# Image 0 loaded as two half transfers on two queues, and seven more idle matmuls, in a one-core attention kernel

## The reference

```
# layer 0
xn  = group_norm(x, eps=1e-5) * gn_scale + gn_bias
q, k, v = split(xn @ w_qkv per head)            # 4 heads of 16 channels
att = softmax(q k^T * 64**-0.5)                 # 256 x 256 per image and head
x   = (att v) @ w_out + b_out + xn
# layer 1
xn  = group_norm(x, eps=1e-3) * gamma + beta
q, k, v = xn @ Wq + bq, xn @ Wk + bk, xn @ Wv + bv
att = softmax(q k^T * 64**-0.5)                 # one head
out = xn + (att v) @ Wp + bp
```

## Time and profile before

| | |
|---|---|
| Three runs | 52.26, 52.64 and 55.1 us, median 52.64 |
| The profiled execution's own time | 52.91 us |
| Its span, first to last instruction | 51.1 us |
| Mean granted TensorE clock | 0.993 of full speed |
| Busy: PE, DVE, ACT, POOL | 89%, 72%, 53%, 35% of the span |
| Input and output | 1.07 MB in all DMAs, 0.72 MB of them read from HBM |

### The profile page before, as it was taken

The page is one execution under the profiler, slowest core; times in us unless marked ns, Lnnn a source line. Parts: engine busy times, 40 slices in busy tenths (PEclk is TensorE's granted clock), DMA queues, the critical chain, the costliest instruction groups (busy, mean ns, idle before and its releaser), DMA issues.

```text
span 51.1 us, 1307 instructions
## 1 busy us (share of the span) xinstructions
PE 45.4 (89%) x459; PEld 38.5 (75%) x459; DVE 36.9 (72%) x102; ACT 27.1 (53%) x63; POOL 18.1 (35%) x44
## 2 busy tenths in 40 slices
PE   2999999789999999599999999995999999999900
PEld 2979979679778497457686687593989999999700
DVE  0047799939926999979999974899489969955330
ACT  0494094506897705910663499672795966343300
POOL 5797637988784000000004450627727000000000
PEclk9999999999999999999999999999999999999997
DMA  0387000000000000000000000000000001010101
GB/s 0 103 228 220 14 0 0 0 0 0 0 13 0 0 0 0 0 6 13 0 0 0 0 0 0 13 0 0 0 0 6 6 0 30 22 51 0 51 13 51
DMA packets 1255, 1.07 MB, mean 21 GB/s; under 512 B 160, under 2 KB 1056, under 8 KB 1248
## 3 DMA queue, kind: packets, MB, share of 16 engines
q1 hardware_dynamic: 1024, 0.82, 5.9%
q10 hardware_dynamic: 224, 0.16, 1.1%
HBM read 0.72 MB, written 0.26 MB: 19 GB/s over the span
## 4 chain that ended last, share of the span: by engine, by line
PE 78%; DVE 7%; ACT 4%; issue 3%; POOL 2%; POOLq 0%; DVEq 0%
PE bank L729 12%; PE bank L761 8%; PE bank L846 7%; PE bank L740 6%; PE bank L720 6%; PE bank L854 6%; PE bank L696 5%; PE bank L835 4%; PE bank L665 4%; PE bank L784 3%; ACT pt L437 3%; PE bank L776 3%; PE bank L816 2%; DVE mv L523 2%; PE bank L817 2%
## 5 line engine op out<-in xcount | busy, mean ns | idle before, releaser
L583 DVE TENSOR_REDUCE nmax<-bank 128x2 fp32r<-128x512 f32 x16 | 10.0, 678 | 2.7 <-PE bank L720 2.7
L437 ACT ACTIVATE pt<-bank 128x512 f32<-128x512 f32 x16 | 8.5, 594 | 5.4 <-PE bank L740 5.4
L333 POOL TENSOR_TENSOR rstd<-mv,half 64x1 f32<-64x1 f32 (+1 forms) x7 | 4.4, 633 | 15.2 <-DVE mv L523 14.8
L729 PE MATMUL bank<-ident,nmax 128*128 128x256 f32 x38 | 7.3, 308 | 0.0
L854 PE MATMUL bank<-idle 128*128 128x128 bf16 x59 | 6.4, 283 | 1.0 <-POOL idle L303 1.0
L729 PEld LDWEIGHTS bank<-ident,nmax 128*128 128x128 f32 x38 | 5.3, 188 | 1.7 <-issue 1.2
L854 PEld LDWEIGHTS bank<-idle 128*128 128x128 bf16 x59 | 5.5, 135 | 1.1 <-POOL idle L303 1.0
L720 PE MATMUL bank<-qk 32*128 32x256 f32 x32 | 3.3, 324 | 1.2 <-ACT pt L437 0.6
L761 PE MATMUL bank<-pt,v 128*32 128x256 f32 x64 | 4.3, 385 | 0.0
L846 PE MATMUL bank<-vn,pt 128*128 128x65 f32 x32 | 4.2, 273 | 0.0
L500 DVE BATCH_NORM_STATS2 bn<-xin 64x6 f32<-64x256 f32 x4 | 1.7, 418 | 3.3 <-DMA xin<-x_dram 3.3
(11 more groups left out here) (104 smaller groups left out, 119.2 us busy)
## 6 DMA issues: line engine op xcount, KB each, us to landing
par<-params_dram SPq DMA_DIRECT2D x1, 288.0 KB, 3.0
out_dram<-res SPq DMA_DIRECT2D x4, 64.0 KB, 1.5
xin<-x_dram SPq DMA_DIRECT2D x1, 128.0 KB, 2.9
par<-params_dram ACTq DMA_DIRECT2D x1, 96.0 KB, 2.9
par<-params_dram SPq DMA_DIRECT2D x1, 64.0 KB, 1.8
xin<-x_dram ACTq DMA_DIRECT2D x1, 64.0 KB, 2.3
xin<-x_dram SPq DMA_DIRECT2D x1, 64.0 KB, 2.7
```

What stands on the lines that cost most here:

```text
L333: nc.gpsimd.tensor_tensor(rstd[:, layer, a:z], mv[:, layer, a:z, 1], half[:, a:z], ALU.pow).then_inc(rstd_ready, 1)
L437: nc.scalar.activation(pt[:, b, h, :, :], bank("T", b, h)[:, :, :], ACT.Exp, scale=SCALE).then_inc(exp_done, 1)
L583: nc.vector.tensor_reduce(nmax[:, b, h, :], bank("S", b, h)[:, :, :], AX_X, ALU.max, negate=True).then_inc(s_max, 1)
L729: pe.matmul(o[:, :, t * HALF:(t + 1) * HALF], nm[:, t:t + 1].broadcast_to([128, 128]), ident[:, :].unsqueeze(1).broadcast_to([128, 2, 128] ...
```

## The change

Image 0 is no longer one transfer of 64 rows on ACT. Its channels 0 to 31 are the first transfer on SP and its channels 32 to 63 are the first on ACT; both add 16 to the same semaphore, so that everyone who waits for image 0 now waits for 32. Block A becomes the second transfer on SP, and images 1, 2 and 3 move back one place each; block B stays second on ACT behind a smaller one; block C still waits for image 0. The slices of image 1 and of images 2 and 3 are written with fewer dimensions. PE's stream gets 2 more idle matmuls between `hop(0)` and `hop(1)` (18 for 16), 1 more ahead of `qk_(0)` (5 for 4) and 4 more ahead of `hop(2)` (10 for 6). Two slices (`qk[:, b, 0:2, :]`, `kl[rows(h), b]`) name the same elements as before.

```diff
+X0_DONE = 32
...
         @block.sync
         def _(sp):
+            sp.dma_start(xin[0:C // 2, 0, :], x[0:C // 2, 0, :]).then_inc(x_in[0], 16)
             sp.dma_start(par[:, 0:END_A], params[:, 0:END_A]).then_inc(a_in, 16)
-            sp.dma_start(xin[:, 1:2, :], x[:, 1:2, :]).then_inc(x_in[1], 16)
-            sp.dma_start(xin[:, 2:B, :], x[:, 2:B, :]).then_inc(x_in[2], 16)
-            sp.wait_ge(x_in[0], 16)
+            sp.dma_start(xin[:, 1, :], x[:, 1, :]).then_inc(x_in[1], 16)
+            sp.dma_start(xin[:, 2:B, :].rearrange("c b n -> c (b n)"), x[:, 2:B, :].rearrange("c b n -> c (b n)")).then_inc(x_in[2], 16)
+            sp.wait_ge(x_in[0], X0_DONE)
             sp.dma_start(par[:, END_B:WIDTH], params[:, END_B:WIDTH]).then_inc(c_in, 16)
...
-                pool.wait_ge(x_in[chain_of(0, b)], 16)
+                pool.wait_ge(x_in[chain_of(0, b)], X0_DONE if b == 0 else 16)
...
-            act.dma_start(xin[:, 0:1, :], x[:, 0:1, :]).then_inc(x_in[0], 16)
+            act.dma_start(xin[C // 2:C, 0, :], x[C // 2:C, 0, :]).then_inc(x_in[0], 16)
...
-                act.wait_ge(x_in[chain_of(0, b)], 16)
+                act.wait_ge(x_in[chain_of(0, b)], X0_DONE if b == 0 else 16)
...
-                nc.scalar.copy(qk[:, b, :, :], bank("QK", b)[:, :, :]).then_inc(qk_hi, 1)
+                nc.scalar.copy(qk[:, b, 0:2, :], bank("QK", b)[:, :, :]).then_inc(qk_hi, 1)
...
-                dve.wait_ge(x_in[chain_of(0, b)], 16)
+                dve.wait_ge(x_in[chain_of(0, b)], X0_DONE if b == 0 else 16)
...
-                               kl[rows(h), b, :] if low else qk[rows(h), b, 1, :], start=(t == 0 and not low),
+                               kl[rows(h), b] if low else qk[rows(h), b, 1, :], start=(t == 0 and not low),
...
-            keep_warm(24); hop(0); keep_warm(16); hop(1); weights_vp(); keep_warm(4); qk_(0); v(0); y_input(0)
-            keep_warm(6); hop(2); keep_warm(7); attend(("S", 0, 0), ("S", 0, 1), ("S", 0, 2), ("S", 0, 3))
+            keep_warm(24); hop(0); keep_warm(18); hop(1); weights_vp(); keep_warm(5); qk_(0); v(0); y_input(0)
+            keep_warm(10); hop(2); keep_warm(7); attend(("S", 0, 0), ("S", 0, 1), ("S", 0, 2), ("S", 0, 3))
```

More of the change, by code:

```diff
@@ L225, in build @@
         dve_step = sem("dve_step")
-        read_by = {"S": s_max, "T": exp_done, "S1": s1_max, "T1": exp1_done, "WV": wvp_ready, "QK": k_ready,
+        read_by = {"S": s_max, "T": exp_done, "S1": s1_max, "T1": exp1_done,
+                   "WV": wvp_ready, "QK": k_ready,
                    "V": v_ready, "HOP": var_ready, "Y": xn1_ready,
```

## The result

The changed kernel takes 55.64 us (median of four executions: 55.43, 55.53, 55.76, 56.18) against 52.67 us before. The ratio is 1.061, with a 95% interval of 1.049 to 1.072. It is slower by 3 us where 0.1 us was forecast; the range ended at 53.5.

The account below looks back on a forecast made before the run. PE, busy 89% of the span, was taken to bound the kernel, with only the start movable. Start +0.12 us, the rest 0: 52.91 to 53.03 us profiled, median 52.76, stated as 52.7; range 52.1 to 53.5 us.

Parts of the forecast that it names:

- which wait takes over: Head of DVE's stream: the wait for block A ends last, swallowing image 0's gain; statistics start 0.12 us later.
- signs of being wrong: Profile signs: DVE idle over 0.3 us before image 1's statistics; idle matmuls' loads still 107 ns after 7.5 us; others.
- Block A was put at 1.17 plus 2.0: Block A second on SP: issued at 1.17, landing at 3.17 us, bounds 2.97 to 4.0.
- Image 1 was put at 4.15: Image 1 third on SP: lands at 4.15 us, half the extra issue's delay; variance of image 0 0.09 us later.
- image 1's slack: DVE ahead of image 0's variance: 0.16 plus 0.19 us of waiting, minus a few hundredths, taken to absorb a later image 1.
- rival D: Start of kernel: both halves and block A land together at about 3.05, image 1 uses its slack; 52.6 us, chance 0.15.
- The rule on partition halves: Splitting image 0: the skill's rule says no gain, later half at 3.05; the rows suggest up to half a microsecond.
- the cover of the idle matmuls at full clock: Seven added idle matmuls on PE: hidden behind other waits, cost 0, bounds 0 and 0.50 us.
- the later first hop: PE's hop of image 0: follows the spread statistics to 4.00 from 3.88, counted as 0.12 us of start delay.
- rival C: PE idles longer before image 0's hop, so its clock rises later: costs 1.46 us, time 54.1 us, chance 0.06.

Follow-up runs that it names:

- r8: Changed kernel with block A first on SP again and half of image 0 second: six executions at 52.68 to 52.95 us, two at 55.73 and 59.85; ratio 1.0038.
- r2: Kernel before with only the change's idle matmuls (18, 5, 10 for 16, 4, 6): 52.70 us, ratio 1.0006.
- r3: Changed kernel with 30 idle matmuls for 24 ahead of the first hop: 52.93, 53.18, 53.20 and 53.30 us, ratio 1.009.
- r12: Kernel before with 22 idle matmuls for 24 ahead of the first hop: two executions at 52.56 and 52.62 us, eight from 55.02 to 59.15 us.
- r1: Changed kernel's transfers with the idle matmuls of before (16, 4, 6): 55.15, 55.16, 58.57 and 59.28 us.
- r9: Changed kernel without DVE's head wait for block A, 26 idle matmuls for 24 before the first hop: seven executions at 52.71 to 53.25 us, three at 54.46 to 55.49.
- r6: Kernel before with 26 idle matmuls for 24 ahead of the first hop: eight executions at 52.43 to 52.74 us, two at 55.19 and 55.29.
- r4: Changed kernel without the wait for block A at the head of DVE's stream: 52.62, 54.33, 55.56 and 59.73 us.
- r5: Kernel before with 20 idle matmuls for 24 ahead of the first hop, no transfer moved: 54.60, 55.49, 58.97 and 59.03 us.

## Why the prediction was wrong

**Right: which wait takes over.** The prediction said that block A would end last at the head of DVE's stream and swallow the gain of image 0. It did; the bracket names `par`. Two of its signs of being wrong came as well: DVE idle for 0.37 us ahead of the statistics of image 1, and weight loads of idle matmuls above 100 ns after 7.5 us.

**Its size was too small.** Block A was put at 1.17 plus 2.0; it took 1.19 plus 2.3 in this execution and 2.0 to 2.3 in the seven traces with these transfers, so the 2.0 was their lower end. Image 1 was put at 4.15, with half of the extra issue counted; it came at 4.55, the full delay and a bit more. So the start cost 0.40 us at the variance for the predicted 0.12, and 0.51 us at the first scores with the gap filled. The halving of the delay because "the bytes ahead of it are the same ones as before" did not hold. Block B is issued sooner now (1.18 for 1.33) and may compete with image 1, but no run separates this. The prediction also took image 1's slack as 0.16 plus 0.19 us: the 0.16 is DVE already waiting for image 1, so only the 0.19 was slack, as its own 0.35 us for a landing at 4.4 has it, and rival D had less room than the 0.35 it counts on.

**The rule on partition halves.** By the Trainium skill, "DMA: Bandwidth & Descriptors", section "Rules for kernel authors", splitting by partition halves brings nothing. In the changed kernel the later half landed at 2.74 for 3.05, and in all seven traces with this order the halves took 1.7 to 2.1 us against 2.2 to 2.4 us for the 64 KB. But this order also moves block A, which was issued beside image 0 before, out of the first place; with A back in it (r8) the later half landed at 3.06, and nothing was left of the gain. So in these runs the 0.3 us came only together with the loss of block A's place. Whether two halves are faster by themselves no run separates. The two inputs that DVE needs together were complete at 3.49 instead of 3.05.

**Right: the cover of the idle matmuls at full clock.** Their cost was taken as 0 with a bound of 0.50; r2 measured 52.70 against 52.67.

**The step that failed: the later first hop was costed as a delay only.** The prediction put the hop 0.12 us later, carried that as 0.12 us of chain, and put its effect on the clock at nothing. Measured, the hop came 0.40 us later, and the clock, which had risen near 6 us, rose near 13 us, which made 2.45 of the 2.97 us (r3). The prediction did have the mechanism as rival C, a longer idle time of PE ahead of the first hop and a later rise, and gave it 0.06. It held against it that "the change adds idle matmuls in just this stretch". They are not in that stretch: all seven stand behind the first hop, while the gap is ahead of it. The three executions of before already held a 55.1, and I named it under rival C without reading it as a sign that the kernel stands at an edge; eight of its 65 executions are beyond it, and eight of ten with 0.2 us more of gap. The two errors belong together: had the hop come only 0.12 us later, the idle time would have been some 0.50 us (an estimate from 0.38), between r8 (0.46, 2 of 8 late) and r12 (0.57, 8 of 10 late), and the median could have fallen on either side.

**Its price was too small as well**, 1.46 us for 2.45. It counted the q and k of image 0 and the first scores at half clock and nothing else. In the trace the first scores ran at full clock; what was slow were the second and third hop, the three small products, q, k, v and the idle matmuls, and all of these turned into the chain, without a break from 4.28 to 13.38. The seven added idle matmuls then lose their cover: at 103 ns each they are 0.72 us (an estimate), and the two faster executions of r1, without them, are at 55.15 for 55.43 us and more. The cover computed for the full clock does not hold at the low one.

Of the clock the Trainium skill says in "TensorE: Matmul & The Clock Gate", Part 1, that the throttled state is the default, that activity of PE releases it, and that the moment varies from run to run. The traces agree: all start with weight loads of idle matmuls at 103 ns and come to about 57 ns, in r9 amid the 18 behind the first hop (79 ns on average), in r3 behind them (111 ns). That the moment varies for one and the same program is seen in the three levels of r12.

Open: what decides whether a single execution is late, so that one program gives all three levels (r12), and what makes executions late of kernels whose traced execution has only 0.26 us (r6) or 0.20 us (r4) of idle time ahead of the first hop. Only traces of several executions of one kernel would tell.

## What to carry to other kernels

Where a kernel holds PE's clock up with idle matmuls, a delay of the first real matmul can cost far more than its own length: ask how long PE now stands idle ahead of it, and extend the idle matmuls ahead of that point, not behind it. Look at all single times, since a few that are 5% longer show that such a kernel is at an edge; here 0.2 us more of idle time made eight of ten executions late, and 0.4 us all four. And before splitting the transfer that ends last, list everything the waiting instruction waits for: here block A, with half a microsecond to spare, gave up its place on the queue and became the last; and with its place kept (r8), the split gained nothing.

## What the runs showed that was not expected

Leaving out four matmuls without use (20 for 24) raised the time from 52.64 us to between 54.6 and 59.0 us. The clock can fall again after it has risen: in r1 it was full from 5.7 to 9.1 us and half until 22.7, with PE busy all that time. The landing of image 1, 64 KB and third on its queue, differed by 0.9 us between executions with the same transfers (3.9 in r4, 4.8 in r9). The profile's granted clock reads full from the start until the first change that it shows: in the first microseconds, when the weight loads of idle matmuls take 103 ns, and in r5 even at 22.6 us, with a mean of 0.999 for an execution that spent its first 22 us at the low clock. The length of a known instruction is the better witness there.
